# Second attention: the third and fourth and the seventh and eighth batches joined into rows of four slots

## The reference, cut to what matters

```python
def _L1_attn_ref(x, gamma, w_qkv, w_out):     # x (2, 1024, 128), after a layernorm
    b, n, _ = x.shape
    xn = rms_norm(x, gamma)
    qkv = (xn @ w_qkv).reshape(b, n, 3, 16, 64)
    q, k, v = jnp.transpose(qkv, (2, 0, 3, 1, 4))
    sim = jnp.einsum('bhid,bhjd->bhij', q * 64 ** -0.5, k)
    attn = jax.nn.softmax(sim, axis=-1)
    out = jnp.einsum('bhij,bhjd->bhid', attn, v)
    out = jnp.transpose(out, (0, 2, 1, 3)).reshape(b, n, 1024)
    return out @ w_out
```

## Time and profile before

| | |
|---|---|
| median of 2 runs | 1058.39 us (1058.34 to 1058.45) |
| the profiled execution's own time | 1057.54 us |
| its span, first to last instruction | 1055.8 us |
| TensorE busy | 1039.9 us, 98% of the span |
| VectorE busy | 787.9 us, 75% |
| GpSimd busy | 784.2 us, 74% |
| ScalarE busy | 563.9 us, 53% |
| granted TensorE clock, mean | 1.000 |

### The profile page before, as it was taken

One profiled execution on the slowest core, in us unless ns is written; L12 is line 12 of the kernel. 1 busy time (PEld: TensorE's weight loads), 2 busy tenths in 40 slices (PEclk: granted clock), 3 DMA queues, 4 the chain that ended last, 5 costly groups with the idle time before them and its releaser, 6 DMA issues.

```text
span 1055.8 us, 22183 instructions
## 1 busy us (share of the span) xinstructions
PE 1039.9 (98%) x8784; PEld 664.3 (63%) x8784; DVE 787.9 (75%) x1239; ACT 563.9 (53%) x912; POOL 784.2 (74%) x514
## 2 busy tenths in 40 slices
PE   9999999999999999999999999999999999999998
PEld 7898898777645545545545545545545545477886
DVE  4658767477777888878878878878878888675554
ACT  5644444555565555555555555555555555544442
POOL 5778998745458898899999999999999999800000
PEclk9999999999999999999999999999999999999999
DMA  7323233543100300000000000000000000000000
GB/s 243 133 82 100 85 122 119 155 139 120 40 1 1 111 1 2 1 1 2 1 1 1 2 1 1 2 1 2 1 2 1 1 1 1 2 0 11 11 1 21
DMA packets 32679, 40.23 MB, mean 38 GB/s; under 512 B 4544, under 2 KB 24384, under 8 KB 31296
## 3 DMA queue, kind: packets, MB, share of 16 engines
q1 hardware_dynamic: 32256, 38.80, 11.4%
q10 hardware_dynamic: 320, 0.01, 0.0%
HBM read 28.97 MB, written 9.70 MB: 37 GB/s over the span
## 4 chain that ended last, share of the span: by engine, by line
PE 80%; DVE 8%; POOL 3%; issue 3%; ACT 3%; DMA 1%; SPq 1%; DVEq 0%; POOLq 0%; ACTq 0%
PE o_ps L1720 18%; PE mx_ps L1673 7%; PE st_ps L1692 5%; PE st_ps L1698 5%; PE st_ps L1695 5%; PE ha_banks L641 5%; PE bank L2149 4%; PE bank L2151 3%; PE bank L2150 3%; PE mx_ps L1610 3%; PE pj_ps L1625 3%; PE mx_ps L1605 3%; PE ha_banks L694 2%; PE ha_banks L705 2%; DVE mx_part L1925 2%
## 5 line engine op out<-in xcount | busy, mean ns | idle before, releaser
L2063 POOL TENSOR_TENSOR acc<-acc,prob 128x1024 f32<-128x1024 f32 x188 | 456.5, 2428 | 34.2 <-POOL acc L2063 23.7
L1863 ACT ACTIVATE prob<-st_ps 128x1024 f32<-128x1024 f32 x256 | 248.3, 1022 | 209.1 <-PE st_ps L1698 106.7
L1720 PE MATMUL o_ps<-prob,v_cur 128*64 128x512 f32 x1024 | 243.4, 596 | 0.0
L1925 DVE TENSOR_REDUCE mx_part<-mx_ps 128x1 f32<-128x512 f32 x258 | 168.0, 678 | 22.4 <-PE mx_ps L1673 13.5
L1720 PEld LDWEIGHTS o_ps<-prob,v_cur 128*64 128x64 f32 x1024 | 69.1, 137 | 120.9 <-issue 80.7
L1928 DVE TENSOR_REDUCE mx_part<-mx_ps 128x2 f32<-128x1024 f32 x78 | 95.6, 1225 | 49.7 <-PE mx_ps L1673 49.7
L1673 PE MATMUL mx_ps<-k_hi,q_hi 64*128 64x512 f32 x414 | 112.1, 457 | 2.5 <-DVE mx_part L1928 0.5
L1698 PE MATMUL st_ps<-q_hi,d_lo 64*128 64x512 f32 x512 | 101.7, 391 | 0.0
L1673 PEld LDWEIGHTS mx_ps<-k_hi,q_hi 64*128 64x128 f32 x414 | 46.9, 183 | 84.8 <-issue 51.1
L2063 POOL TENSOR_TENSOR acc<-prob 128x1024 f32<-128x1024 f32 x32 | 76.6, 2393 | 23.6 <-ACT prob L1863 23.6
L949 POOL TENSOR_TENSOR ha_wide<-ha_pt,ha_own 128x512 f32<-128x512 f32 x64 | 74.4, 1186 | 9.4 <-ACT ha_pt L905 9.2
(11 more groups left out here) (393 smaller groups left out, 2157.5 us busy)
## 6 DMA issues: line engine op xcount, KB each, us to landing
w_tile<-w_rows SPq DMA_DIRECT2D x72, 128.0 KB, 2.9
v_rows<-ha_v SPq DMA_DIRECT2D x8, 1024.0 KB, 4.1
ha_vt<-v_rows SPq DMA_DIRECT2D x16, 512.0 KB, 4.2
q_max<-mx_turned SPq DMA_DIRECT2D x128, 1.0 KB
h_w<-in_h SPq DMA_DIRECT2D x2, 1024.0 KB, 8.3
w_raw<-in_w SPq DMA_DIRECT2D x8, 192.0 KB, 4.0
head_wkv<-in_wkv SPq DMA_DIRECT2D x2, 512.0 KB, 4.7
m_w<-in_m SPq DMA_DIRECT2D x3, 256.0 KB, 3.0
```

The source lines that it names most:

```text
L1720: mm = pe.matmul(o_ps[rows(h), :], v_cur[:, m % 2, j, rows(h)], prob[:, (16 * m + slot) % RING, h, :], start=(j == 0), stop=(j == KT - 1), ...
L1863: act.activation(prob[:, n % RING, :, :], st_ps[:, slot % 2, :, :], ACT.Exp, scale=SCALE).then_inc(s_exp, 1)
L1925: dve.reduce_max(mx_part[:, h, i, keys:keys + 1], maxima_banks(q, n)[h], AX_X).then_inc(s_mxr, 1)
L2063: pool.tensor_tensor(total, old, new, ALU.add).then_inc(s_acc, 2)
```

## The change

`JOINS = (2, 6)` joins batch 2 with 3 and batch 6 with 7, wherever `three` holds for both. Such a pair is issued as one: four slots' scores with the four maxima between them, then units and values. ScalarE takes four Exps, then the copies. VectorE takes the four maxima's reductions, then low parts and denominators. The waits are adapted: the second pair's unit waits for the first one to have left bank 1, and the third maxima wait only for the reduction of bank 0. GpSimd's order is unchanged.

```diff
+    JOINS = (2, 6)
...
+    def joined(m, b):
+
+        return b in JOINS and three(m, b) and three(m, b + 1)
...
         elif aside(q, u):
 
-            pe.wait_ge(s_mxr, all_out[maximum(q - AHEAD[u], BEFORE.index(u), 0)])
+            m, b = q - AHEAD[u], BEFORE.index(u)
+            pe.wait_ge(s_mxr, all_out[maximum(m, b + 1 if joined(m, b) else b, 0)])
+            if joined(m, b - 1) and before(m, b - 1):
+                unit_out(pe, *before(m, b - 1))
...
+        elif n % 2 and joined(*batch_before(q, n)):
+
+            pe.wait_ge(s_mxr, first_out[divmod(16 * q + n - 1, 16)])
...
+    def tensor_two(pe, m, b):
+        tensor_maxima(pe, *maximum(m, b, 0))
+        tensor_scores(pe, m, 2 * b)
+        tensor_scores(pe, m, 2 * b + 1)
+        tensor_maxima(pe, *maximum(m, b, 1))
+        tensor_scores(pe, m, 2 * b + 2)
+        tensor_maxima(pe, *maximum(m, b + 1, 0))
+        tensor_scores(pe, m, 2 * b + 3)
+        tensor_maxima(pe, *maximum(m, b + 1, 1))
+        if before(m, b):
+            tensor_unit(pe, *before(m, b))
+        tensor_outputs(pe, m, 2 * b - 2)
+        tensor_outputs(pe, m, 2 * b - 1)
+        if before(m, b + 1):
+            tensor_unit(pe, *before(m, b + 1))
+        tensor_outputs(pe, m, 2 * b)
+        if after(m, b):
+            tensor_unit(pe, *after(m, b))
+        tensor_outputs(pe, m, 2 * b + 1)
+        if after(m, b + 1):
+            tensor_unit(pe, *after(m, b + 1))
...
+    def scalar_two(act, m, b):
+        for slot in range(2 * b, 2 * b + 4):
+            scalar_exp(act, m, slot)
+        for i in (b, b + 1):
+            if before(m, i):
+                scalar_unit(act, *before(m, i))
+        for i in (b, b + 1):
+            if after(m, i):
+                scalar_unit(act, *after(m, i))
...
+    def vector_two(dve, m, b):
+        vector_maxima(dve, *maximum(m, b, 0))
+        was = (m, b - 1)
+        if after(*was) and after(*was)[1][0] == "out":
+            vector_add_out(dve, *after(*was))
+        vector_maxima(dve, *maximum(m, b, 1))
+        vector_maxima(dve, *maximum(m, b + 1, 0))
+        vector_maxima(dve, *maximum(m, b + 1, 1))
+        for i in (b, b + 1):
+            if before(m, i) and before(m, i)[1][0] == "qk":
+                vector_low(dve, *before(m, i))
+            if den_at(DEN_SUM, m, i):
+                vector_den_sum(dve, *den_at(DEN_SUM, m, i))
+        for i in (b, b + 1):
+            if den_at(DEN_BACK, m, i):
+                vector_den_back(dve, *den_at(DEN_BACK, m, i))
+            if den_at(NORMALIZE, m, i):
+                vector_normalize(dve, *den_at(NORMALIZE, m, i))
```

More of the change, by code:

```diff
@@ L1508, in aside @@
         return three(q - AHEAD[u], b)
+    runs = [(m, b, 2 if joined(m, b) else 1) for m in range(STEPS + 1) for b in range(BATCHES)
+            if b == 0 or not joined(m, b - 1)]
     turns = [(0, QK[3]), (0, ("v", 0)), (0, ("v", 1)), (0, QK[2])]
[L1512 to L1517, removed]
+    pj_uses = turns[:]
+    for m, b, size in runs:
+        of = range(b, b + size)
+        later = [after(m, i) for i in of] + [u for i in of for u in norm_at(m, i)]
+        turns += [u for u in [before(m, i) for i in of] + later if u]
+        pj_uses += [u for u in [maxima_there(m, i) for i in of] + [unit_there(m, i) for i in of] + later
+                    if u and u[1] != ("norm", "mean")]
     turn_of = {turn: n for n, turn in enumerate(pj_uses)}
@@ L1755, in tensor_begin @@
         tensor_maxima(pe, 0, 10)
-    def tensor(pe, m, b):
+    def tensor_two(pe, m, b):
[19 more added lines that the diff above has]
+            tensor_unit(pe, *after(m, b + 1))
+    def tensor(pe, m, b):
+        if joined(m, b):
+            tensor_two(pe, m, b)
+            return
+        if joined(m, b - 1):
+            return
         first, second = maximum(m, b, 0), maximum(m, b, 1)
@@ L1851, in scalar_begin, with scalar_exp @@
         scalar_unit(act, 0, QK[2])
-    def scalar(act, m, b):
+    def scalar_exp(act, m, slot):
+        n = 16 * m + slot
+        act.wait_ge(s_st, n + 1)
+        if n >= RING:
+            old = n - RING
+            act.wait_ge(s_pv, old + 1)
+            act.wait_ge(s_acc, 2 * (ADDS * (old // 16) + 7 * (old % 16 // KT) + max(1, old % KT)))
+        act.activation(prob[:, n % RING, :, :], st_ps[:, slot % 2, :, :], ACT.Exp, scale=SCALE).then_inc(s_exp, 1)
+    def scalar_two(act, m, b):
[7 more added lines that the diff above has]
+                scalar_unit(act, *after(m, i))
+    def scalar(act, m, b):
+        if joined(m, b):
+            scalar_two(act, m, b)
+            return
+        if joined(m, b - 1):
+            return
         if m < STEPS:
             for slot in (2 * b, 2 * b + 1):
[L1856 to L1863, removed]
+                scalar_exp(act, m, slot)
         names = NORMS_AT.get((m, b), ())
@@ L1999, in vector_begin @@
         vector_maxima(dve, 0, 10)
-    def vector(dve, m, b):
+    def vector_two(dve, m, b):
[16 more added lines that the diff above has]
+                vector_normalize(dve, *den_at(NORMALIZE, m, i))
+    def vector(dve, m, b):
+        if joined(m, b):
+            vector_two(dve, m, b)
+            return
+        if joined(m, b - 1):
+            return
         first, second = (maximum(m, b, i) if m or b else None for i in range(2))
```

6 lines of the change are left out of this document (4 added, 2 removed).

## The result

The joined kernel takes 1071.88 us (median of 2 runs, 1071.0 to 1072.77) against 1058.39 before, a ratio of 1.0131 with a 95% interval of 1.0109 to 1.0153: 1.3% slower. The forecast was 1073.0. The profiled execution's span grew from 1055.8 to 1069.2 us.

What follows compares the result with a forecast made beforehand. TensorE, busy 98% of the span, was taken to bound the kernel. Net losses of 0.60 (b=2) and 0.44 us (b=6), 1.04 per step, over 14 steps add 14.6 to 1058.4: 1073.0 us; 8-in-10 range 1062 to 1081.

Steps and rivals of the forecast that it cites:

- 1, third slot's scores on the Exp: In the joined row, the third slot's scores wait for the first slot's Exp to release their bank: 0.35 us.
- 2, restart: First FP32R pair after a wait costs 0.10 us more, bounds 0 and 0.10; here at the third slot's scores.
- 3, fourth slot's scores: Fourth slot's scores need the second slot's Exp released; no wait was expected, with 0.1 us to spare.
- 4, fourth maxima on the reduction: Fourth maxima wait for the third maxima's first reduction, same `mx_ps` bank 0: 0.23 us, allowing 0.1 less or more.
- 4, restart: The fourth maxima's first FP32R pair, after their wait, costs 0.10 us more.
- 5, unit on the second reduction (b=2): At b=2 the unit waits for the third maxima's second reduction, both using bank 1: 0.18 us.
- saved (what is left): Fewer changes between FP32 and FP32R, a cheaper denominators' product and a lost unit wait: 0.36 us (b=2), 0.34 (b=6).
- The thin cover of the second unit: Batch 3's unit waits for the queries' low part to leave bank 1; expected covered with 0.14 us to spare.
- its four chances: Chances given: forecast 0.78, waits staying hidden 0.07, VectorE becoming the bound 0.12, clock falling 0.02.
- the first rival: The joined row's waits stay hidden and only the saving is left: 9.8 us less, 1048.6; chance 0.07.
- VectorE did not become the bound: Rival: VectorE's late subtraction delays the second unit and next reductions, half a microsecond per b=2 pair, 1080 us; chance 0.12.
- The clock did not fall: Rival: short waits in the joined rows halve TensorE's clock in one pair in ten, 31 us, 1104; chance 0.02.

## Why the prediction was right

The forecast of 1073.0 was met within 1.1 us, through the mechanism it names: a bank's release comes later than the cover in the row, once at the Exp and once at the reduction. Three of its terms were off, two beyond the bounds that it gave, and that they cancel is luck. Per pair, in us, from the distances of starts:

| step of the forecast | forecast | measured, b=2 | measured, b=6 |
|---|---|---|---|
| 1, third slot's scores on the Exp | 0.35 | 0.36 | 0.36 |
| 2, restart | 0.10 | 0.11 | 0.10 |
| 3, fourth slot's scores | none | none | none |
| 4, fourth maxima on the reduction | 0.23 | 0.46 | 0.31 |
| 4, restart | 0.10 | 0.11 | 0.10 |
| 5, unit on the second reduction (b=2) | 0.18 | none | |
| lost | 0.96, 0.78 | 1.04 | 0.87 |
| saved (what is left) | 0.36, 0.34 | 0.53 | 0.37 |
| net | +0.60, +0.44 | +0.51 | +0.50 |

- *Waits 1 to 3.* Right to 0.01. The sum of scores-to-Exp 0.20, Exp 1.02 and release 0.05 was all it needed. Of the cover of 0.1 us for the fourth slot enough remained.
- *Wait 4* is the term that was mis-sized. I gave every release 0.05 us, read from a unit with one wait. With three waits in front it took 0.10 at b=6, and with four 0.26 at b=2; with the extra ones issued earlier 0.05 at both. The bound of 0.1 more did not hold 0.46.
- *Wait 5* did not come, and for that very reason: the maxima were so late that the second reduction was over. Forecast 0.41 for waits 4 and 5 together, measured 0.46. The longer wait in front swallowed the one behind it, as the Exp's wait had swallowed that of the third maxima until the Exps were cut.
- *Savings.* The denominators' product between FP32 groups costs 0.09, not 0.24, so 0.29 were saved and not 0.14, which was also the upper bound. But 0.21 of the 0.38 was no price of the product or of the change of kind; it was the wait for the low part, which the joined order took away by putting scores in its place. With the maxima pair (0.07), the change back (0.09) and the unit's wait (0.06) that makes 0.51 of the 0.53. At b=6 the sum of 0.34 was right to 0.03.
- *The thin cover of the second unit* held: it starts 1.72 after the values, as reckoned, and 0.18 after the end of the low part it needs.
- *The sum.* 1.01 us a step where 1.04 was forecast, and 14 steps grew by 14.1 us (568.08 to 553.97, the latter from 337.98 to 891.95). The rest of the program gave 0.7 us back. The errors of wait 4, wait 5 and the denominators were each 0.15 to 0.23 us and of both signs, so by luck the sum is better than its terms. The range of the forecast had a slip too: its high end of 1.48 a step leaves out the 0.1 more that wait 4 was allowed at each of the two pairs, 1.68 with it, 1082. And its four chances add up to 0.99, not 1.
- *The rivals.* The waits did not stay hidden; with the Exps and reductions cut they do, and then 4.3 us are gained, not the 9.8 of the first rival. VectorE did not become the bound, though its busy time rose by 24 us: each pair alone costs what it costs beside the other. The clock did not fall: the granted clock is 1.00 in the three stretches, through 28 rows with at least two waits each. The section on psum-queue depth-cycling in the Trainium skill, "TensorE: Matmul & The Clock Gate", that the forecast weighed tells of another kernel whose clock swung with such short idle times; this trace does not show it.
- *What would show it.* Pairs of 11.3 and 10.0 (11.24, 10.09), the gap of 0.35 and unjoined batches as long as now were right; 0.23 and 0.18 were not; and there are not 28 fewer first pairs of 0.50, since a pair that follows a wait looks like one (350.15 and 370.64 in the second step).

## What to carry to other kernels

In a row of work on a saturated engine, count for each resource in the ring (score banks, maxima banks) the time from its last writer to its release by the reader, and the engine's own work in between: a row that joins two batches keeps the saving of the changes of kind only as far as that work covers the release. Taking one of several waits in series away is worth only its lead over the next one, so cut two at once before you judge either. And keep a control with the same cut in the kernel before; here it had a wait of its own.

## What the runs showed of the hardware

- Semaphores that were met long ago still cost time when they stand with a late one in front of the same matmul: the start came 0.05 us after the reduction's end with one wait or with the others out of the way, 0.10 with three waits and 0.26 with four. The maxima behind the low part, which have two waits, started 0.15 after its end. The 0.26 were the same with the reductions cut; TensorE came 0.20 after the release there, and 0.06 and a restart were left. The trace has instructions of 0.05 us that only wait, two of them behind the release at b=2, one that is through with it at b=6. How the waits stand among each other was not varied.
- After a wait the first pair of FP32R products takes 0.31 to 0.34 us up to the next start where 0.23 is usual, as after FP32 work, and a pair in front of a unit 0.42 to 0.43 where it is 0.32.
- A wait can hide in the duration of the short instruction before it: 0.38 us up to the next start for a product that takes 0.09 between others and 0.17 in front of maxima that don't wait. The table of waits named it only once the product was moved away.
- A multiplication on VectorE of two tiles took 0.68 us by itself, and when it began well before the end of an add of GpSimd it ended 0.55 us after that add, after up to 2.8 us. The same normalization so took 1328 ns on average in one order and 1955 ns in the other. This is read from the 32 of each trace; no run varied it.
